# A head's queries and keys loaded by one transfer each, repeated by a zero stride, in three attentions

## The reference, cut to what matters

```
x = x + rotary_attention(layernorm(x))            # 16 heads of 8
x = x + experts(layernorm(x))                     # one shared and 7 routed experts, top 2
x = x + attention_block(layernorm(x))             # 16 heads of 8, own norm, biases, residual
x = x + relative_attention_then_moe(layernorm(x)) # 16 heads of 8, 32 experts, top 4
```

```
scores = einsum('bqhd,bkhd->bhqk', q, k) * scale
attn = softmax(scores, axis=-1)
out = einsum('bhqk,bkhd->bqhd', attn, v)
```

## Time and profile before

| | us |
|---|---|
| median of three runs | 2145.89 |
| the profiled execution | 2154.38 |
| its span | 2152.2 |
| TensorE matmuls, busy in the span | 2002.8 (93%) |
| VectorE busy | 1415.1 (66%) |
| ScalarE busy | 1198.3 (56%) |
| GpSimd busy | 511.2 (24%) |
| mean granted TensorE clock | 0.944 of full speed |

### The profile page before, as it was taken

How to read it: one execution, slowest core, us unless ns; L and a number is a source line. 1 busy time by engine, 2 the same in 40 slices (tenths; PEclk the granted TensorE clock), 3 DMA queues, 4 the chain that set the end, 5 groups by cost and what they waited for, 6 DMA issues and landing times. The chain is left out here.

```text
span 2152.2 us, 43028 instructions
## 1 busy us (share of the span) xinstructions
PE 2002.8 (93%) x13792; PEld 1204.8 (56%) x13792; DVE 1415.1 (66%) x1857; ACT 1198.3 (56%) x2297; POOL 511.2 (24%) x495
## 2 busy tenths in 40 slices
PE   5999999779996899999768999999999999986998
PEld 2344444457774344444346666666666666664887
DVE  6899999356656899999566455455455545435776
ACT  2688888446662488888523444444444444443554
POOL 2000000048883000000122222222222222102664
PEclk8799999789997699999779999999999999997999
DMA  8444543121102544444161112111221112013564
GB/s 271 122 111 116 124 113 92 50 85 61 60 20 83 160 111 118 123 112 111 57 178 44 47 46 66 48 46 45 54 57 48 46 45 63 12 31 140 216 218 149
DMA packets 90287, 198.95 MB, mean 92 GB/s; under 512 B 19888, under 2 KB 49328, under 8 KB 84784
## 3 DMA queue, kind: packets, MB, share of 16 engines
q1 hardware_dynamic: 90224, 198.15, 32.2%
HBM read 163.47 MB, written 36.18 MB: 93 GB/s over the span
## 5 line engine op out<-in xcount | busy, mean ns | idle before, releaser
L1157 DVE TENSOR_REDUCE M<-PS 128x1 f32<-128x1024 f32 x512 | 599.4, 1220 | 59.3 <-PE PS L610 59.3
L1428 ACT ACTIVATE PR<-PS 128x512 f32<-128x512 f32 x1024 | 535.9, 590 | 115.6 <-PE PS L630 114.7
L1467 ACT ACTIVATE PR<-PS 128x512 f32<-128x512 f32 x512 | 306.1, 598 | 377.4 <-PE PS L739 373.5
L1178 DVE TENSOR_REDUCE M<-PS 128x1 f32<-128x1024 f32 x256 | 311.9, 1222 | 219.5 <-PE PS L725 212.4
L630 PE MATMUL PS<-Qs_r,Ks_r 32*128 32x512 f32 x1024 | 380.9, 512 | 1.7 <-ACT PR L1428 1.4
L640 PE MATMUL PS<-PR,Va 128*32 128x256 f32 x4096 | 326.4, 404 | 0.0
L610 PE MATMUL PS<-Ks_r,Qs_r 32*128 32x512 f32 x1024 | 268.1, 521 | 16.9 <-DVE M L1157 10.9
L610 PEld LDWEIGHTS PS<-Ks_r,Qs_r 32*128 32x128 f32 x1024 | 99.6, 191 | 198.1 <-issue 127.1
L630 PEld LDWEIGHTS PS<-Qs_r,Ks_r 32*128 32x128 f32 x1024 | 153.1, 187 | 93.1 <-ACT PR L1428 69.2
L1173 DVE TENSOR_TENSOR rt<-PS,rel 128x512 f32<-128x512 f32 x128 | 88.5, 691 | 155.4 <-PE PS L697 153.9
L1601 POOL TENSOR_TENSOR Va<-Vt,nil 128x64 f32<-128x64 f32 x96 | 27.9, 294 | 610.6 <-PE PS L640 601.0
(11 more groups left out here) (196 smaller groups left out, 3096.1 us busy)
## 6 DMA issues: line engine op xcount, KB each, us to landing
Qs_r<-q_stack SPq DMA_DIRECT2D x384, 128.0 KB, 2.6
Ks_r<-k_stack SPq DMA_DIRECT2D x384, 128.0 KB, 3.1
Qs<-g_dram SPq DMA_DIRECT2D x30, 1024.0 KB, 4.8
o_dram<-Ob SPq DMA_DIRECT2D x96, 128.0 KB, 2.5
Ks<-g_dram SPq DMA_DIRECT2D x10, 1024.0 KB, 4.9
q_stack<-hl SPq DMA_DIRECT2D x18, 256.0 KB, 3.2
k_stack<-hl SPq DMA_DIRECT2D x18, 256.0 KB, 3.9
q_stack<-PR_r SPq DMA_DIRECT2D x18, 256.0 KB, 3.3
```

Of the source, the lines that this page charges most:

```text
L1157: e.tensor_reduce(M[:, s, qt:qt + 1], PS[:, 2 + 2 * (qt % 2):4 + 2 * (qt % 2), :] .rearrange("p a b -> p (a b)"), AX.X, ALU.max, negate=Tr ...
L1178: e.tensor_reduce(M[:, s, qt:qt + 1], PS[:, bk:bk + 2, :].rearrange("p a b -> p (a b)"), AX.X, ALU.max, negate=True).then_inc(max_done, 1)
L1428: e.activation(PR[:, kt % 4, qh * GW:(qh + 1) * GW], bank(RING[(x if x < 4 else x + 1) % 3]), ACT.Exp, scale=SCALE).then_inc(exp_done, 1)
L1467: e.activation(PR[:, kt % 4, qh * GW:(qh + 1) * GW], bank(TURN[kt % 2][qh]), ACT.Exp)\
```

## The change

Each of the two groups of four transfers becomes one, whose destination is all 128 partitions of the slot. Its source is the head's [32, 1024] stack with a leading dimension of 4 and a stride of zero. The thresholds of the waits on qk_in go from 8 x 16 = 128 per load to 2 x 16 = 32.

```
 def load_qk(n, s):
     for to, of in ((Qs_r, q_stack), (Ks_r, k_stack)):
-        for r in range(4):
-            e.dma_start(to[r * KR:(r + 1) * KR, s, :].bitcast(F32), of[bass.ds(n, 1)].rearrange("n r t -> (n r) t"))\
-                .then_inc(qk_in[s], 16)
+        e.dma_start(to[:, s, :].bitcast(F32),
+                    of[bass.ds(n, 1)].broadcast_to([4, KR, L])).then_inc(qk_in[s], 16)
...
-                                e.wait_ge(qk_in[s2], 128 * (NH // SLOTS * a + block + (s >= 2) + 1))
+                                e.wait_ge(qk_in[s2], 32 * (NH // SLOTS * a + block + (s >= 2) + 1))
...
-                    e.wait_ge(qk_in[n], 128 * (NH // SLOTS * a + 1))
+                    e.wait_ge(qk_in[n], 32 * (NH // SLOTS * a + 1))
...
-                        e.wait_ge(qk_in[s], 128 * (2 * NH // SLOTS + block + 1))
+                        e.wait_ge(qk_in[s], 32 * (2 * NH // SLOTS + block + 1))
```

## The result

The changed kernel takes **2698.88 us** (median of four runs, 2693.48 to 2702.83) against 2147.03 us for the kernel before, run beside it: a ratio of 1.256, with a 95% interval of 1.253 to 1.259. It is 552 us slower. The forecast was 3122 us in a range from 2480 to 3430.

What follows compares the result with a forecast made beforehand. TensorE, busy 93% of the span, was taken as the bound, no attention waiting for loads. Added terms 263 + 265 + 36 + 356 + 56 = 976 us on the median of 2145.9 gave 3122 us, range 2480 to 3430.

Steps and rivals of the forecast that it cites:

- 920 us of waits: All three attentions: 263 us longer in attention 0, 265 in attention 1, and 36 plus 356 in attention 2.
- 56 us for the clock: Attention 2: after each of 28 pauses, 4 us at half speed lose 2.0 us; nothing taken for attentions 0 and 1.
- The number of engines: Each load transfer: the outermost count sets how many of 16 DMA engines take part; the source's 4 gives 4 engines.
- the mechanism in attention 2: Each of 28 positions waits at its prep, as the load outlasts its room: 12.7 us each, 356 us.
- The price of a load: Time to move one head's 1.05 MB on 4 engines: 17.4 us, with ends of 11.2 and 20.2.
- the fixed part: Each load: time from issue to first data and from last data to the semaphore, 2.1 us.
- the first rival: All attentions: four engines at the fast rate, a load taking 11.2 us, period 11.8 in attentions 0 and 1; 2524 us, chance 0.18.
- Attentions 0 and 1: the wrong regime: Loads queue back to back on four engines, so a period of 18.0 us per head instead of 10.2: +263 and +265 us.
- the room of 6.9 us: Attention 2: time from a load's issue to the prep of the same head, in a position of 24.3 us.
- The later start: Attention 2: the first prep of head 2 waits until load 2 has landed, +36 us.
- What I had taken as unchanged: Attentions 0 and 1, from position 29 on, after load 31: nothing differs from the kernel before.
- The second: Rival, all loads: all 16 engines take the transfer by the destination's 128; -3 us, at most some -12, 2143 us, chance 0.09.

Runs made afterwards that it cites:

- e1_count4: The kernel before, its eight transfers a head kept without zero stride, each source read as 4 outermost times 8 rows: 2611.63 us, ratio 1.2145.
- e3_two_copies: The changed kernel with two transfers of two copies each for queries and for keys, so a zero-stride count of 2: 3463.63 us in a single run.
- e8_count8: The kernel before, its eight transfers a head kept, each source read as 8 outermost times 4 rows: 2287.72 us, ratio 1.0655.
- e2_rows128: The changed kernel's single transfers reading 128 different rows, without zero stride; heads mixed, softmax left out: 2153.77 us, ratio 1.0010 to the kernel before.
- e6_rows_act: The changed kernel with the max rows of attentions 0 and 1 issued by ScalarE on its own queue instead of SP: 2686.06 us, ratio 1.2489.
- e5_filler: The changed kernel with 26 extra unused matmuls ahead of each wait for a load in attention 2: 2633.19 us, ratio 1.224.

## Why the prediction was right, and its sizes not

**In one view.** The prediction had 920 us of waits and 56 us for the clock; measured are 374 and 172. The number of engines, the sign and the mechanism in attention 2 were right. The price of a load was too high, the fixed part and the clock too low, and the errors partly cancel. With the measured D of 10.3 us my own sums, those of the first rival, give about 2460 us (an estimate: 46 us longer for each of attentions 0 and 1, 222 for attention 2), below the bottom of my range. That the measured time lies inside the range is in part luck.

**The number of engines: right.** Four, by the small packets, and e1_count4, e3_two_copies and e8_count8 show counts of 4, 2 and 8 taking 4, 2 and 8 engines with and without a zero stride. e2_rows128 shows that the size of a transfer and its 128 partitions cost nothing.

**The price of a load, D: the step that failed.** I took 17.4 us, at the rate of the earlier trace rows, "as its packets are the same 4 KB rows from the same tensors". It is 10.3 us. The nearest row by tensor was not the nearest by what limited it: that window was transfers onto 32 partitions each. The same rows move at 346 GB/s in e2_rows128, 21.6 KB/us for each of 16 engines. Even the fast end of 23.5 KB/us was under the 25.5 that four engines reach. The estimate of 19.3 us by the Trainium skill's port rule ("SBUF — State Buffer", "Door 1: The DMA port swizzle") lies far above the measured 10.3 as well; four engines carried 102 GB/s, where two ports of 27.2 GB/s would allow 54. Either their rows don't go to two ports, or the rule doesn't bind here; no run tells these apart.

**The fixed part of a load: too small.** I took 2.1 us. In attention 2 the timeline shows a load from its issue to its use:

```profile
1506.48 0.62 SPq L362 DMA_DIRECT2D Qs_r<-q_stack  x1
...
1514.02 0.38 SPq L381 DMA_DIRECT2D o_dram<-Ob  x1
...
1520.85 0.78 PE L696 MATMUL PS<-Qs_r,Ws_r 32*128 32x512 f32 x1 [6.89 <-DMA Ws_r<-w_stack]
```

14.4 us from issue to use. The load with Ws_r (2 KB an engine) and the store (8 KB) is 272 / 25.5 = 10.7 of it, which leaves 3.7. Of these, 1.5 us pass before the first packet and 0.5 us between the last packet and TensorE's start, which is close to my 2.1. About 1.0 us more is the slow first half of the load, which e1_count4 doesn't have, and the rest is the last microsecond, in which the engines end one after another. I had not counted the store as being in front of the load's end here.

**Attentions 0 and 1: the wrong regime.** With D + 3.7 = 14.0 instead of 19.5, the queue isn't always full. A position that waits and one that doesn't alternate, as my first rival had it. Its formula gave 11.8 us (12.0 with the store, which it left out); measured are 14.2 and 13.8. SP's timeline in attention 0 shows a pair, with TensorE's return between:

```profile
290.49 0.62 SPq L362 DMA_DIRECT2D Qs_r<-q_stack  x1
...
300.67 0.62 SPq L362 DMA_DIRECT2D Qs_r<-q_stack  x1
...
306.48 0.80 PE L609 MATMUL PS<-Ks_r,Qs_r 32*128 32x512 f32 x2 [5.42 <-DMA Qs_r<-MT]
...
317.80 0.61 SPq L362 DMA_DIRECT2D Qs_r<-q_stack  x1
```

The pair is 27.3 us: 16.0 from the issue to TensorE's return, of which 10.2 lie beside the position before, and a position of 11.3. I had 13.3 and 10.2 for these two. Of the 16.0, D and the 3.7 explain 14.0; the other 2.0 stay open, and e6_rows_act shows that they aren't the max rows' place in the queue. The position after a wait is longer for the clock, which I had priced at nothing there; over 306.4 to 318.1 us it was 0.80, in the next position, without a wait, 1.00:

```profile
306.40:318.10 11.70, 11.06 (x98) 4.44 (x99) 8.86 (x8) 8.46 (x18) 0.29 (x1) 0.80 0.22 87
318.10:328.20 10.10, 10.10 (x102) 4.14 (x98) 9.29 (x9) 8.56 (x19) 0.29 (x1) 1.00 0.26 86
```

That nothing was a second mistake: the clock costs 91 us in these two attentions, a third of what they lose.

**Attention 2: right in kind.** A wait in each of 28 positions, by the room of 6.9 us: 7.2 us instead of 12.7. The clock after it: 2.7 us instead of 2.0, of which e5_filler gives 2.2 back. The later start: 11.4 us (from load 0 to load 3) instead of 36. Up to load 31 that makes 278 us, and 288 with the last position, where I had 448.

**The rest.** 33.5 us lie outside these stretches. 32 of them are the positions after load 31: from its issue to the end of the loop the changed kernel takes 6.4, 16.4 and 9.3 us longer in attentions 0, 1 and 2. The first of these positions waits for load 31, which my sums included. What I had taken as unchanged are those behind it, and in attention 1 they aren't. Over its last two whole positions TensorE waits for no transfer and is busy nearly all the time, yet they take 15.2 and 15.1 us instead of 9.9 and 9.8:

```profile
1272.30:1302.60 30.30, 29.75 (x176) 10.06 (x177) 8.68 (x9) 18.36 (x37) 0.00 (x0) 0.50 0.04 12
```

The clock had fallen in the wait of 4.9 us before them and stayed at 0.50 for these 30 us of dense work. My 4 us of half speed after a pause is thus no upper bound.

**The rivals.** The first, four engines at the fast rate (0.18), was the nearest mechanism: 2524 us against 2699, short by the fixed part and the clock. The second, 16 engines, didn't come; e2_rows128 shows what it would have been: no change.

## What to carry to other kernels

Before merging transfers, look at the outermost count of both sides: a zero-stride repetition in front of the rows put the transfer on as few engines as there were copies (4 and 2 here), which one can count by a transfer's small packets. Then hold the new time to landing, its fixed part included, against the room from issue to use; issues that nobody waits for are worth nothing, here eight in place of two for each head. And don't take an engine's rate from a window in which something else may set the pace; take it from one with few engines at work, and leave room above the highest rate that any row shows (23.5 KB/us against a measured 25.5). Where a wait is forecast, price the clock behind it too: here it was a third of the loss.

## What the runs showed of the hardware

- Four engines carry 102 GB/s (25.5 KB/us each), two 52 GB/s (e3_two_copies, 500 to 504 us), 16 engines by transfers onto 32 partitions 241 GB/s, or 15.1 KB/us each at 92% busy, and by transfers onto 128 partitions 346 GB/s, 21.6 KB/us each at 89% busy (e2_rows128).
- With three loads queued on four engines, their issuer is held up as well. At the start of attention 1 SP needed 5.9 and 5.2 us for one issue each, against 0.6 in the loop, and 7.2 for three stores, against 1.8 in the kernel before:

```profile
830.33 5.87 SPq L362 DMA_DIRECT2D Qs_r<-q_stack  x1
836.24 5.19 SPq L362 DMA_DIRECT2D Ks_r<-k_stack  x1
841.48 7.17 SPq L332 DMA_DIRECT2D q_stack<-PR_r  x3
```

- A wait of 2.5 us in positions of 28.5 was enough to bring the mean granted clock of attention 2 from 1.00 to 0.95 (e8_count8), and 26 useless matmuls ahead of a longer wait brought it from 0.86 to 0.99 and the kernel 66 us down (e5_filler). After the last wait of attention 1 the clock stayed at 0.50 for 30 us in which TensorE was 98% busy.
